# Shifted values copied as 112 rows and the rest, and the first batch's norm and turn by halves

## The chip, the cores and the metric

The kernel runs on one core of a Trainium2 chip. The time is the device time of one execution in microseconds (us); lower is better. In the core, TensorE (PE, with its weight load PEld), VectorE (DVE), ScalarE (ACT) and GpSimd (POOL) each run their own queue of instructions in order. SyncE (SP) issues all the DMAs here. The queues wait for each other through semaphores, which the kernel writes by hand.

## The reference

x is 4 batches of 1024 tokens of 128 channels, in float32. Cut to what matters here:

```python
h  = layernorm(x)
a  = h + ripple(h, Wqkv, Wo, conv_w)        # attention
x  = x + layernorm(a)
x  = x + layernorm(ffn(layernorm(x)))       # 8 experts, top 2, and a shared one

# ripple, per head of 16 channels (8 heads):
q, k, v = split(h @ Wqkv)
offsets = [0, 1, 2, 4, 8, 16, 32, 64, 128, 256, 512]    # earlier tokens that exist
w    = softmax over the offsets of q[s] . k[s - off] / 4
tele = sum over the offsets of w[off] * v[s - off]
conv = causal depthwise convolution of v, 7 taps
low  = elu features: fq @ (fk^T v) / (fq . sum fk)
out  = (tele + conv + low) @ Wo
```

The term `tele` needs, for each token s, the values of the tokens s - 1, s - 2, up to s - 64. The change touches how these shifted values are fetched, and how the first `layernorm(x)` of batch 0 is computed.

## The kernel before, in words

Tokens lie in 8 tiles of 128: tile j has its 128 tokens on the 128 partitions, so `x_in`, `xn`, `v_tok` are [128, 8, 128] (partition, tile, channel), 4 KB in each partition. Channel-major copies ([128 channels, 1024 tokens]) have names that end in T: `xnT`, `kT`, `qT`, `vT`.

**Batch by batch.** Each engine runs a loop over b = 0 to 4. In turn b the attention of batch b is computed, and beside it the feed-forward part of batch b-1 by units u of 512 tokens, and the normalising, turning and projecting of batch b+1. Batch 0 has no feed-forward beside it, so its stretch (about 19 to 87 us of the trace) is the attention of batch 0 and the preparation of batch 1.

**The start.** SP issues `x_in` first. DVE's `stats(0)` (L739, L743) takes mean and variance of the 8 tiles, POOL's `ln1(0)` turns them into `rstd1` by a power (L420) and into `nmr1` (L429), ACT's `normalise1(0)` (L502) writes `xn` in 8 instructions. PE's `turn_x` (L1081) transposes 4 tiles into each half of the PSUM tile `psA`; ACT's `evacuate_x` (L490) copies each half to `xnT`; PE projects k, q and v (L1089), each in two halves through the same `psA`, and ACT evacuates each. Before `turn_x(0)` PE runs 28 transposes that keep it busy (L1275). DVE's next work after `stats(0)` is `products(0, 0)` (L260), which waits for `qT`.

**The shifted values.** A token's value 1 to 64 tokens earlier lies on another partition, which the engines can't reach in an elementwise operation. So, once `v_tok` of a batch is evacuated, SP copies it by DMA from SBUF to SBUF into `v_shift` [128, 7, 8, 128], one slot for each offset in `SHIFTS` = 1, 2, 4, 8, 16, 32, 64 (`shift_v`, L333 to L337). For an offset `off` one DMA moves 128 - off partitions down by `off` (L336), 4 KB for each partition, and a second one takes the last `off` partitions of each tile to the first `off` partitions of the next tile (L337):

```python
sp.dma_start(v_shift[off:P, n], v_tok[0:P - off]).then_inc(v_shifted, 16)
sp.dma_start(v_shift[0:off, n, 1:NT], v_tok[P - off:P, 0:NT - 1]).then_inc(v_shifted, 16)
```

That is 14 DMAs and 3.60 MB in a batch. All of them count on one semaphore, and DVE waits for the full count once in each batch, ahead of the first tile of `weigh` (j = 0, L840). `weigh` multiplies the values by the softmax weights, tile by tile, into a ring of 4 buffers (`terms`); PE's `sum_terms` (L1166, L1169) sums them in `psH`, `add_conv` (L871, DVE) adds the convolution after tiles 4 and 7, PE applies `Wo` (L1180). DVE reaches `weigh` after products, features, convolution (`convolve`, L862, L864) and softmax of the batch.

**SP's queue.** Its order is fixed: in turn b the load of `x_in` for b+1, the 14 shift copies of b, a store, the reload of `x_res`, a store. Nothing that comes later is issued while an earlier issue stalls.

Of the kernel before, what the change touches and what calls it, by code (L numbers as in the profile page):

```python
# [16 lines left out]
ALU = mybir.AluOpType  # L17
# [3 lines left out]
P = 128  # L21
# [23 lines left out]
SHIFTS = TERMS[M_SHIFT:M_LOW]  # L45
# [7 lines left out]


N_DMA = 16
N_SHIFT_DMA = 16 * 2 * len(SHIFTS)
N_PSA_FULL, N_PSA_FREE = 16, 14

PSA_V_TOK, PSA_FK_TOK, PSA_SCORES, PSA_SCORES_T, PSA_X, PSA_K, PSA_Q, PSA_V = range(8)
PSA_AHEAD = 2 * 4  # L60
N_PRODUCTS = (4, 8, 11)
N_SOFTMAX_STEPS = 5
N_CONV_STEPS = TAPS

N_FRONT = 3
# [47 lines left out]
def block_kernel(nc, x, Wqkv, Wo, conv_w, gate_W, W1, b1, W2, b2, Ws1, bs1, Ws2, bs2, route_scale, out):  # L113
# [4 lines left out]
    with ExitStack() as ctx:  # L118
# [6 lines left out]
        def sem(name):  # L125
            return ctx.enter_context(nc.semaphore(name))
# [14 lines left out]
        neg_half = sb("neg_half", [P, NT])  # L141
# [11 lines left out]
        x_in = sb("x_in", [P, NT, P])  # L153
# [149 lines left out]
        def _(sp):  # L303
# [28 lines left out]
            def shift_v(b):  # L332

                sp.wait_ge(psA_free, freed(b, PSA_V_TOK, 1))
                for n, off in enumerate(SHIFTS):
                    sp.dma_start(v_shift[off:P, n], v_tok[0:P - off]).then_inc(v_shifted, 16)  # L336
                    sp.dma_start(v_shift[0:off, n, 1:NT], v_tok[P - off:P, 0:NT - 1]).then_inc(v_shifted, 16)  # L337

            def store(u):
# [24 lines left out]
        def _(pool):  # L364
# [51 lines left out]
            def rstd_of(var, src, scale, rstd, step, value, cols):  # L416

                nc.gpsimd.tensor_scalar(var[:, cols], src, scale, EPS, ALU.mult, ALU.add).then_inc(step, 1)  # L418
                pool.wait_ge(step, value)
                return nc.gpsimd.tensor_tensor(rstd[:, cols], var[:, cols], neg_half[:, cols], ALU.pow)  # L420

            def ln1(b):
                pool.wait_ge(stats1, upto(b, 1, 1))
                if b >= 3:
                    pool.wait_ge(ln3_ready, 2 * (b - 2))
                nc.gpsimd.tensor_scalar(neg_mean[:, b % 3, :], mv[:, :, 0], -1.0, 0.0, ALU.mult, ALU.add)
                rstd_of(var1, mv[:, :, 1], 1.0, rstd1, ln1_step, upto(b, 2, 1), slice(0, NT)).then_inc(ln1_step, 1)
                pool.wait_ge(ln1_step, upto(b, 2, 2))
                nc.gpsimd.tensor_tensor(nmr1[:], neg_mean[:, b % 3, :], rstd1[:], ALU.mult).then_inc(ln1_ready, 1)  # L429

            def ln2(u):
# [24 lines left out]
                nc.gpsimd.tensor_tensor(y_out[:, tiles, :], y_out[:, tiles, :], x2[:, tiles, :],  # L456
                                        ALU.add).then_inc(out_ready[0], TPH)

            ln1(0)
            constants()  # L460
            more_constants()
            for b in range(B + 1):
# [25 lines left out]
        def _(act):  # L488
# [6 lines left out]
                copy(dst, psA[:, half, :]).then_inc(psA_free, 1)  # L495

            def normalise1(b, tiles=range(NT)):
                act.wait_ge(ln1_ready, upto(b, 1, 1))
                if b:
                    act.wait_ge(xn_kept, upto(b - 1, 1, 1))  # L500
                for j in tiles:
                    nc.scalar.activation(xn[:, j, :], x_in[:, j, :], ACT.Identity, bias=nmr1[:, j:j + 1],  # L502
                                         scale=rstd1[:, j:j + 1]).then_inc(xn_ready, 1)

# [6 lines left out]
            def evacuate_x(b):  # L511
                for half in range(2):
                    evacuate(b - 1, PSA_X, half, xnT[:, bass.ts(half, HALF)])
# [214 lines left out]
        def _(dve):  # L728
# [4 lines left out]
            nc.vector.memset(hid[32:HID, 4, :], 0.0)  # L733
            nc.vector.memset(ksum_sel[:], 0.0).then_inc(zeros_set, 1)

            def stats(b):
                dve.wait_ge(x_in_ld, upto(b, N_DMA, 16))
                for j in range(NT):
                    last = nc.vector.bn_stats(bn[:, j, :], x_in[:, j, :])  # L739
                last.then_inc(bn_done, 1)  # L740
                dve.wait_ge(bn_done, upto(b, 1, 1))
                for j in range(NT):
                    last = nc.vector.bn_aggr(mv[:, j, :], bn[:, j, :])  # L743
                last.then_inc(stats1, 1)
# [661 lines left out]
```

## Time and profile before

| | |
|---|---|
| median of 3 runs | 334.6 us (333.72 to 335.88) |
| profiled execution | 334.57 us, its span 332.9 us |
| DVE busy | 269.8 us, 81% of the span |
| PE, PE load | 253.2 us, 172.3 us |
| ACT, POOL | 176.6 us, 72.1 us |
| mean granted clock of TensorE | 0.892 of full speed |
| data moved by DMA | 21.88 MB, mean 66 GB/s |

All the views show one profiled execution; 1.7 us of its time lie outside the span. The page's fourth part follows the chain of work that ended last back from the last instruction, and gives its share by line. A timeline gives each group of instructions with start, length and the idle time of its engine before it, with what ended that (`<-`). "SPq" is SP's queue: its rows are the issues of DMAs, not the transfers. In the view by stretches, PEclk is the granted clock of TensorE (1.00 is 2.4 GHz, 0.50 is 1.2 GHz), and the DMA share is the mean busy share of the core's 16 DMA engines: one engine of sixteen busy all the time is 0.06.

### The profile page before, as it was taken

How to read it: one execution, taken by the hardware profiler on the slowest of the kernel's cores; microseconds unless marked ns; L12 is line 12 of the kernel's file. 1: busy time of each engine (PE TensorE's matmuls, PEld its weight loads, DVE VectorE, ACT ScalarE, POOL GpSimd, SP SyncE). 2: the span in 40 equal slices, each digit the busy share in tenths (PEclk: the TensorE clock that was granted, in tenths of full speed). 3: DMA queues.
4: the chain of work that ended last, by engine and by line, in shares of the span. 5: the costliest groups of instructions: out<-in, count | busy, mean ns of one | idle time of the engine just before them, and what ended most of it. 6: DMA issues, size and time to landing. Idle time of an engine off the chain costs nothing.

```text
span 332.9 us, 4518 instructions
## 1 busy us (share of the span) xinstructions
PE 253.2 (76%) x1527; PEld 172.3 (52%) x1527; DVE 269.8 (81%) x595; ACT 176.6 (53%) x443; POOL 72.1 (22%) x129
## 2 busy tenths in 40 slices
PE   6668772088589939997898469997797588878894
PEld 6324340087436615776655228767444266675374
DVE  5079996088997999979989999889989989855752
ACT  1683256002536945584769625785478306176851
POOL 4903000001091000302492000221910003131013
PEclk9787979559959987999999959999999569999999
DMA  8200368000024720030038510100248301000003
GB/s 225 70 0 17 99 170 184 26 3 3 4 67 125 213 77 16 0 95 3 19 111 201 156 44 2 32 2 6 78 123 207 103 17 32 0 2 1 1 2 95
DMA packets 20037, 21.88 MB, mean 66 GB/s; under 512 B 3289, under 2 KB 16434, under 8 KB 20014
## 3 DMA queue, kind: packets, MB, share of 16 engines
q1 hardware_dynamic: 20014, 21.59, 23.5%
q8 instruction: 12, 0.20, 0.2%
q14 instruction: 11, 0.09, 0.1%
HBM read 5.07 MB, written 2.10 MB: 22 GB/s over the span
## 4 chain that ended last, share of the span: by engine, by line
PE 32%; DVE 22%; SPq 14%; ACT 12%; DMA 10%; POOL 4%; issue 3%; POOLq 0%; DVEq 0%; ACTq 0%
DMA v_shift<-v_tok 9%; SPq L337 9%; PE psH L1169 7%; PE psA L1089 6%; SPq L336 6%; DVE convT L864 5%; DVE prods L840 3%; PE psY L1266 3%; PE psF L1230 3%; PE psY L1180 2%; POOL rstd L420 2%; ACT xn L576 2%; DVE hid L968 2%; POOL var L418 2%; PE psA L1081 2%
## 5 line engine op out<-in xcount | busy, mean ns | idle before, releaser
L418 POOL TENSOR_SCALAR var<-ss 128x4 f32<-128x4 f32 (+1 forms) x25 | 13.2, 527 | 233.9 <-ACT squares L621 113.6
L260 DVE TENSOR_TENSOR prods<-qT,kT 128x1024 f32<-128x1024 f32 (+1 forms) x44 | 48.8, 1165 | 12.5 <-ACT qT L490 12.5
L1169 PE MATMUL psH<-ident,prods 128*128 128x128 f32 x324 | 42.8, 284 | 0.0
L1169 PEld LDWEIGHTS psH<-ident,prods 128*128 128x128 f32 x324 | 39.0, 148 | 2.3 <-issue 2.3
L420 POOL TENSOR_TENSOR rstd<-var,neg_half 128x4 f32<-128x4 f32 (+2 forms) x29 | 37.8, 1302 | 2.4
L840 DVE TENSOR_TENSOR prods<-v_shift,wgt 128x896 f32<-128x896 f32 x32 | 34.6, 1083 | 0.0
L864 DVE SCALAR_TENSOR_TENSOR convT<-vT,cw,convT 128x1024 f32<-128x1024 f32 x24 | 30.8, 1284 | 0.7
L1137 PE MATMUL psA<-prods,slot_sel 128*32 128x512 f32 x168 | 25.9, 671 | 7.3 <-DVE prods L260 5.3
L840 DVE TENSOR_TENSOR prods<-v_tok,wgt 128x128 f32<-128x128 f32 (+2 forms) x60 | 21.9, 391 | 11.6 <-DMA v_shift<-v_tok 11.6
L1089 PE MATMUL psA<-xnT,wqkv 128*128 128x512 f32 x48 | 28.8, 742 | 3.3 <-ACT xnT L490 3.3
L1230 PE MATMUL psF<-x3T,w 128*128 128x512 f32 x58 | 31.0, 647 | 0.1
L968 DVE TENSOR_TENSOR hid<-hid,psG 128x512 f32<-128x512 f32 x32 | 20.8, 683 | 8.3 <-PE psG L1252 7.3
L1166 PE MATMUL psH<-ident,prods 128*128 128x128 f32 x32 | 9.7, 304 | 20.8 <-DVE prods L840 17.2
L1252 PE MATMUL psG<-gT,gate_sel 24*128 24x512 bf16 x32 | 11.7, 421 | 17.2 <-DVE hid L968 15.7
L563 ACT ACTIVATE squares<-yc 128x128 f32<-128x128 f32 x32 | 9.4, 296 | 27.8 <-DVE yc L877 27.8
L598 ACT ACTIVATE hid<-psF,b1c 128x512 f32<-128x512 f32 x29 | 18.8, 685 | 2.8 <-PE psF L1230 2.7
L1266 PEld LDWEIGHTS psY<-w,hid 128*128 128x128 f32 x140 | 17.5, 205 | 4.2 <-DVE prods L824 3.6
L1266 PE MATMUL psY<-w,hid 128*128 128x128 f32 x140 | 17.7, 289 | 1.7 <-DVE prods L824 1.7
L1166 PEld LDWEIGHTS psH<-ident,prods 128*128 128x128 f32 x32 | 4.7, 147 | 26.5 <-DVE prods L840 21.6
L1089 PEld LDWEIGHTS psA<-xnT,wqkv 128*128 128x128 f32 x48 | 10.2, 237 | 15.2 <-ACT xnT L490 5.8
L1230 PEld LDWEIGHTS psF<-x3T,w 128*128 128x128 f32 x58 | 10.6, 205 | 13.5 <-issue 12.7
L502 ACT ACTIVATE xn<-x_in,nmr,rstd 128x128 f32<-128x128 f32 x32 | 12.9, 484 | 7.1 <-POOL nmr L429 7.1
(192 smaller groups left out, 520.3 us busy)
## 6 DMA issues: line engine op xcount, KB each, us to landing
x_in<-L_attn_x SPq DMA_DIRECT2D x4, 512.0 KB, 3.8
x_res<-L_attn_x SPq DMA_DIRECT2D x4, 512.0 KB, 15.6
v_shift<-v_tok SPq DMA_DIRECT2D x4, 508.0 KB
v_shift<-v_tok SPq DMA_DIRECT2D x4, 504.0 KB
v_shift<-v_tok SPq DMA_DIRECT2D x4, 496.0 KB
v_shift<-v_tok SPq DMA_DIRECT2D x4, 480.0 KB
v_shift<-v_tok SPq DMA_DIRECT2D x4, 448.0 KB
out<-y_out SPq DMA_DIRECT2D x7, 256.0 KB, 2.3
```

The lines of the kernel that those rows point to most:

```text
L260: return eng.tensor_tensor(prods[:, QUADS * (s % 2) + q, t0:T], qT[:, t0:T], kT[:, PRE - off + t0:PRE - off + T], ALU.mult)
L336: sp.dma_start(v_shift[off:P, n], v_tok[0:P - off]).then_inc(v_shifted, 16)
L337: sp.dma_start(v_shift[0:off, n, 1:NT], v_tok[P - off:P, 0:NT - 1]).then_inc(v_shifted, 16)
L420: return nc.gpsimd.tensor_tensor(rstd[:, cols], var[:, cols], neg_half[:, cols], ALU.pow)
L840: return nc.vector.tensor_tensor(dst, src.rearrange("p m (h d) -> p m h d", d=HD), w, ALU.mult)
L864: conv_chain(nc.vector.scalar_tensor_tensor(out=convT[:], in0=v, scalar=w, in1=convT[:], op0=ALU.mult, op1=ALU.add))
L968: nc.vector.tensor_tensor(hid[:, c, cols], hid[:, c, cols], psG[:, c % 2, :], ALU.mult).then_inc(gated, 1)
L1089: pe.matmul(psA[:, half, :], wqkv[:, bass.ts(part, P)], xnT[:, bass.ts(half, HALF)], start=True, stop=True).then_inc(psA_full, 1)
L1137: ins = pe.matmul(psA[32 * q:32 * q + 32, half, :], ksum_sel[:] if low else slot_sel[:, s, :], fqT[:, cols] if low else prods[:, QUADS * ( ...
L1169: ins = pe.matmul(dst, terms[:, j % TERM_BUFS, m, :], ident[:], is_transpose=True, start=False, stop=(m == live[-1]))
L1230: pe.matmul(hidden_bank(u, c), w1[:, bass.ts(c, P)], x3T[:, half_cols(u)], start=True, stop=True).then_inc(hidden_full, 1)
L1266: ins = pe.matmul(output_tile(u, n), hid[:, c, bass.ts(j, P)], w2[:, c, :], start=(c == CH - 1), stop=(c == CH - 2))
```

## The change

Two parts.

**The shift copies.** Where an offset leaves more than 112 partitions to move (offsets 1, 2, 4 and 8), the first of its DMAs is cut into one of 112 partitions and one of the rest (15, 14, 12 or 8). Offset 16 has 112, and 32 and 64 have fewer, so they stay. A batch has 18 copies in place of 14, of the same bytes; the count that DVE waits for is raised with them.

**The first batch's norm.** DVE's `first_norm` replaces `stats(0)`: by halves of 4 tiles it takes the statistics and adds epsilon (`var1`), POOL takes only the power of each half (`first_rstds`), DVE computes `nmr1` of each half and later `neg_mean`, and ACT normalises each half when its `nmr1` is there. DVE, not ACT, copies the two halves of the turned x from PSUM to `xnT`. Batches 1 to 3 are normalised as before, with the counts on their semaphores moved down by one.

```diff
-N_SHIFT_DMA = 16 * 2 * len(SHIFTS)
+SHIFT_ROWS = 112
+N_SHIFT_DMA = 16 * sum(3 if P - off > SHIFT_ROWS else 2 for off in SHIFTS)
@@ SP, shift_v
                 for n, off in enumerate(SHIFTS):
-                    sp.dma_start(v_shift[off:P, n], v_tok[0:P - off]).then_inc(v_shifted, 16)
+                    rows = min(SHIFT_ROWS, P - off)
+                    sp.dma_start(v_shift[off:off + rows, n], v_tok[0:rows]).then_inc(v_shifted, 16)
+                    if off + rows < P:
+                        sp.dma_start(v_shift[off + rows:P, n], v_tok[rows:P - off]).then_inc(v_shifted, 16)
                     sp.dma_start(v_shift[0:off, n, 1:NT], v_tok[P - off:P, 0:NT - 1]).then_inc(v_shifted, 16)
@@ POOL
+            def first_rstds():
+                for half in range(2):
+                    cols = slice(half * TPH, (half + 1) * TPH)
+                    pool.wait_ge(first_var, half + 1)
+                    nc.gpsimd.tensor_tensor(rstd1[:, cols], var1[:, cols], neg_half[:, cols],
+                                            ALU.pow).then_inc(first_rstd, 1)
...
-            ln1(0)
+            first_rstds()
             constants()
@@ ACT
             def normalise1(b, tiles=range(NT)):
-                act.wait_ge(ln1_ready, upto(b, 1, 1))
                 if b:
+                    act.wait_ge(ln1_ready, upto(b - 1, 1, 1))
                     act.wait_ge(xn_kept, upto(b - 1, 1, 1))
                 for j in tiles:
+                    if b == 0 and j % TPH == 0:
+                        act.wait_ge(first_normed, j // TPH + 1)
...
             normalise1(0)
-            evacuate_x(0)
+            act.wait_ge(psA_free, freed(-1, PSA_X, 1))
             evacuate_k(0)
@@ DVE
+            def first_norm():
+
+                dve.wait_ge(x_in_ld, N_DMA)
+                first_chain.start(dve, 0)
+                for half in range(2):
+                    tiles = range(half * TPH, (half + 1) * TPH)
+                    cols = slice(half * TPH, (half + 1) * TPH)
+                    for j in tiles:
+                        last = nc.vector.bn_stats(bn[:, j, :], x_in[:, j, :])
+                    first_chain(last)
+                    for j in tiles:
+                        last = nc.vector.bn_aggr(mv[:, j, :], bn[:, j, :])
+                    first_chain(last)
+                    nc.vector.tensor_scalar(var1[:, cols], mv[:, cols, 1], EPS, None, ALU.add).then_inc(first_var, 1)
+                for half in range(2):
+                    cols = slice(half * TPH, (half + 1) * TPH)
+                    dve.wait_ge(first_rstd, half + 1)
+                    nc.vector.scalar_tensor_tensor(out=nmr1[:, cols], in0=mv[:, cols, 0], scalar=-1.0,
+                                                   in1=rstd1[:, cols], op0=ALU.mult,
+                                                   op1=ALU.mult).then_inc(first_normed, 1)
+                nc.vector.tensor_scalar(neg_mean[:, 0, :], mv[:, :, 0], -1.0, None, ALU.mult)
+                for half in range(2):
+                    dve.wait_ge(psA_full, filled(-1, PSA_X, half))
+                    nc.vector.tensor_copy(xnT[:, bass.ts(half, HALF)], psA[:, half, :]).then_inc(psA_free, 1)
...
-            stats(0)
+            first_norm()
             dve.wait_ge(consts_ready, 1)
```

SP's queue from the load of batch 1's `x_in` on, before (127x1024 is 127 partitions of 1024 float32):

```order
L326 DMA x_in<-L_attn_x 128x8x128
L336 DMA v_shift<-v_tok 127x1024
L337 DMA v_shift<-v_tok 1x16x56
L336 DMA v_shift<-v_tok 126x1024
L337 DMA v_shift<-v_tok 2x896
```

and with the change:

```order
L331 DMA x_in<-L_attn_x 128x8x128
L342 DMA v_shift<-v_tok 112x1024
L344 DMA v_shift<-v_tok 15x1024
L345 DMA v_shift<-v_tok 1x16x56
L342 DMA v_shift<-v_tok 112x1024
L344 DMA v_shift<-v_tok 14x1024
L345 DMA v_shift<-v_tok 2x896
L342 DMA v_shift<-v_tok 112x1024
```

The copy of 127 partitions is now one of 112 and one of 15, that of 126 one of 112 and one of 14; the small copies behind them are as they were.

DVE's queue from its last memset to the features of batch 0, before:

```order
L734 MEMSET ksum_sel 128x32
L739 BN_STATS bn<-x_in 128x6 x8
L743 BN_AGGR mv<-bn 128x2 x8
L260 TENSOR_TENSOR prods<-qT,kT 128x1024 x4
L765 SCALAR_TENSOR_TENSOR fkT,ksum<-kexp,fkT 128x1024
```

and with the change (`nmr` is `nmr1`, `var` is `var1`):

```order
L751 MEMSET ksum_sel 128x32
L761 BN_STATS bn<-x_in 128x6 x4
L764 BN_AGGR mv<-bn 128x2 x4
L766 TENSOR_SCALAR var<-mv 128x4
L761 BN_STATS bn<-x_in 128x6 x4
L764 BN_AGGR mv<-bn 128x2 x4
L766 TENSOR_SCALAR var<-mv 128x4
L770 SCALAR_TENSOR_TENSOR nmr<-mv,rstd 128x4 x2
L773 TENSOR_SCALAR neg_mean<-mv 128x8
L776 COPY xnT<-psA 128x512 x2
L265 TENSOR_TENSOR prods<-qT,kT 128x1024 x4
L807 SCALAR_TENSOR_TENSOR fkT,ksum<-kexp,fkT 128x1024
```

DVE has seven instructions more ahead of the products: two `var`, two `nmr`, one `neg_mean` and two copies to `xnT`. The statistics come in groups of four tiles.

## Rows read from the trace of the kernel before

**Rows 1.** The page: busy time of each engine, and the chain by line.
```profile
PE 253.2 (76%) x1527; PEld 172.3 (52%) x1527; DVE 269.8 (81%) x595; ACT 176.6 (53%) x443; POOL 72.1 (22%) x129
...
DMA v_shift<-v_tok 9%; SPq L337 9%; PE psH L1169 7%; PE psA L1089 6%; SPq L336 6%; DVE convT L864 5%; DVE prods L840 3%; PE psY L1266 3%; PE psF L1230 3%; PE psY L1180 2%; POOL rstd L420 2%; ACT xn L576 2%; DVE hid L968 2%; POOL var L418 2%; PE psA L1081 2%
```

**Rows 2.** Timeline of DVE (start us, us, engine, line, tiles, idle before).
```profile
55.01 0.68 DVE L824 TENSOR_TENSOR prods<-psY,wgt 128x512 f32<-128x512 f32 x1
66.59 0.29 DVE L840 TENSOR_TENSOR prods<-v_tok,wgt 128x128 f32<-128x128 f32 x1 [10.90 <-DMA v_shift<-v_tok]
...
75.52 0.69 DVE L871 TENSOR_TENSOR prods<-psH,convT 128x512 f32<-128x512 f32 x1 [1.48 <-PE psH L1169]
...
269.56 0.29 DVE L840 TENSOR_TENSOR prods<-v_tok,wgt 128x128 f32<-128x128 f32 x1 [0.71 <-DMA v_shift<-v_tok]
```

**Rows 3.** Timeline of SP's queue, batch 0: the shift copies' issues.
```profile
25.97 0.73 SPq L336 DMA_DIRECT2D v_shift<-v_tok  x1
26.74 8.11 SPq L337 DMA_DIRECT2D v_shift<-v_tok  x1
...
50.44 1.05 SPq L337 DMA_DIRECT2D v_shift<-v_tok  x1
```

**Rows 4.** Stretches: length, busy us of each engine, PEclk, DMA share, GB/s.
```profile
core 0: us, PE busy (x) PEld busy (x) DVE busy (x) ACT busy (x) POOL busy (x), PEclk, DMA share, GB/s
13.30:16.50 3.20, 3.20 (x7) 1.37 (x6) 0.00 (x0) 1.23 (x3) 3.06 (x21) 0.61 0.56 164
28.00:34.80 6.80, 4.45 (x36) 2.42 (x32) 6.73 (x14) 0.81 (x1) 2.64 (x4) 0.89 0.07 26
50.40:55.70 5.30, 1.77 (x4) 0.30 (x2) 5.12 (x7) 4.65 (x6) 0.00 (x0) 1.00 1.06 230
57.70:66.50 8.80, 0.00 (x0) 0.00 (x0) 0.00 (x0) 0.00 (x0) 0.00 (x0) 0.50 0.06 26
66.70:74.50 7.80, 6.56 (x34) 6.56 (x35) 7.34 (x14) 0.00 (x0) 0.00 (x0) 0.54 0.01 3
89.50:97.50 8.00, 4.82 (x21) 1.38 (x21) 7.96 (x22) 4.81 (x21) 6.04 (x8) 0.59 0.07 22
```

**Rows 5.** DVE's convolution, 36 to 44 us and 48 to 57 us (busy, mean ns).
```profile
L864 DVE SCALAR_TENSOR_TENSOR convT<-vT,cw,convT 128x1024 f32<-128x1024 f32 x2 | 2.6, 1284 | 0.1
...
L864 DVE SCALAR_TENSOR_TENSOR convT<-vT,cw,convT 128x1024 f32<-128x1024 f32 x2 | 2.6, 1285 | 0.1
```

**Rows 6.** Timeline of the start, all engines.
```profile
3.06 6.13 PE L1275 MATMUL psG<-ident 128*128 128x128 f32 x28 [3.06 <-POOL ident L374]
...
4.24 1.64 DVE L739 BATCH_NORM_STATS2 bn<-x_in 128x6 f32<-128x128 f32 x8 [0.69 <-DMA x_in<-L_attn_x]
...
5.92 0.64 DVE L743 BATCH_NORM_AGGREGATE mv<-bn 128x2 f32<-128x6 f32 x8
...
7.20 1.66 POOL L420 TENSOR_TENSOR rstd<-var,neg_half 128x8 f32<-128x8 f32 x1
...
9.18 3.19 ACT L502 ACTIVATE xn<-x_in,nmr,rstd 128x128 f32<-128x128 f32 x8 [7.11 <-POOL nmr L429]
...
10.97 0.64 PE L1081 MATMUL psA<-ident,xn 128*128 128x128 f32 x4 [1.78 <-ACT xn L502]
...
12.42 1.11 PE L1081 MATMUL psA<-ident,xn 128*128 128x128 f32 x4 [0.81 <-ACT xn L502]
...
18.28 0.60 ACT L490 ACTIVATE qT<-psA 128x512 f32<-128x512 f32 x1 [0.36 <-PE psA L1089]
...
19.02 4.63 DVE L260 TENSOR_TENSOR prods<-qT,kT 128x1024 f32<-128x1024 f32 x4 [12.46 <-ACT qT L490]
```

**Rows 7.** Timeline of POOL: two powers of four columns.
```profile
81.29 1.19 POOL L420 TENSOR_TENSOR rstd<-var,neg_half 128x4 f32<-128x4 f32 x1
...
91.76 1.86 POOL L420 TENSOR_TENSOR rstd<-var,neg_half 128x4 f32<-128x4 f32 x1
```

**Rows 8.** Waits of the whole span: us in total, times, longest.
```profile
DVE prods L840 <- DMA v_shift<-v_tok: 11.6, 2, 10.9
```

More of the change, by code:

```diff
@@ L62 @@
 N_SOFTMAX_STEPS = 5
+N_FIRST_STEPS = 4
 N_CONV_STEPS = TAPS
@@ L228, in block_kernel @@
         bn_done = sem("bn_done")
+        first_step, first_var = sem("first_step"), sem("first_var")
+        first_rstd, first_normed = sem("first_rstd"), sem("first_normed")
         ln1_ready, ln2_ready, ln3_ready, ln4_ready = sem("ln1_ready"), sem("ln2_ready"), sem("ln3_ready"), sem("ln4_ready")
@@ L250, in block_kernel @@
         softmax_chain = Chain(softmax_step, N_SOFTMAX_STEPS)
+        first_chain = Chain(first_step, N_FIRST_STEPS)
         conv_chain = Chain(conv_step, N_CONV_STEPS)
@@ L420, in rstd_of @@
                 return nc.gpsimd.tensor_tensor(rstd[:, cols], var[:, cols], neg_half[:, cols], ALU.pow)
+            def first_rstds():
[4 more added lines that the diff above has]
+                                            ALU.pow).then_inc(first_rstd, 1)
             def ln1(b):
-                pool.wait_ge(stats1, upto(b, 1, 1))
+                pool.wait_ge(stats1, upto(b - 1, 1, 1))
                 if b >= 3:
@@ L426, in ln1 @@
                 nc.gpsimd.tensor_scalar(neg_mean[:, b % 3, :], mv[:, :, 0], -1.0, 0.0, ALU.mult, ALU.add)
-                rstd_of(var1, mv[:, :, 1], 1.0, rstd1, ln1_step, upto(b, 2, 1), slice(0, NT)).then_inc(ln1_step, 1)
-                pool.wait_ge(ln1_step, upto(b, 2, 2))
+                rstd_of(var1, mv[:, :, 1], 1.0, rstd1, ln1_step, upto(b - 1, 2, 1), slice(0, NT)).then_inc(ln1_step, 1)
+                pool.wait_ge(ln1_step, upto(b - 1, 2, 2))
                 nc.gpsimd.tensor_tensor(nmr1[:], neg_mean[:, b % 3, :], rstd1[:], ALU.mult).then_inc(ln1_ready, 1)
@@ L734, in _ @@
             nc.vector.memset(ksum_sel[:], 0.0).then_inc(zeros_set, 1)
+            def first_norm():
[21 more added lines that the diff above has]
+                    nc.vector.tensor_copy(xnT[:, bass.ts(half, HALF)], psA[:, half, :]).then_inc(psA_free, 1)
             def stats(b):
-                dve.wait_ge(x_in_ld, upto(b, N_DMA, 16))
+                dve.wait_ge(x_in_ld, upto(b, N_DMA, N_DMA))
                 for j in range(NT):
@@ L740, in stats @@
                 last.then_inc(bn_done, 1)
-                dve.wait_ge(bn_done, upto(b, 1, 1))
+                dve.wait_ge(bn_done, upto(b - 1, 1, 1))
                 for j in range(NT):
```

## The prediction

> **What bounds the kernel now.** I read the page first. DVE is the busiest engine, 81% of the span, and on the chain that ended last the transfers to `v_shift` have 9% and their issues on SP (L336, L337) another 15% [rows 1]. So the next question is where DVE waits for them. The view of waits gives two such waits and 11.6 us for the whole program [rows 8]; the timeline of DVE places them. In batch 0 DVE is through with its last work ahead of `weigh` at 55.69 (55.01 + 0.68) and starts the first tile at 66.59, after 10.90 us of idling. In batch 3 it idles 0.71 us at the same place, in batches 1 and 2 not at all [rows 2].
>
> Then the transfers themselves. SP issues the first copy of batch 0 at 25.97 and the last at 50.44, and one issue alone takes 8.11 us [rows 3]: the queue stalls. The view by stretches tells why. From 28.0 to 34.8 and again from 57.7 to 66.5 the DMA share is 0.07 and 0.06, one engine of sixteen, and 26 GB/s move. In between, from 50.4 to 55.7, all engines are busy and 230 GB/s move. Batch 1 shows the same thin stretch at 89.5 to 97.5 [rows 4]. A copy of 127 partitions is 127 x 4 KB = 0.52 MB; at 26 GB/s it takes 20 us. That fits one engine carrying all of the copy for offset 1, first alone with the queue blocked behind it, and at the end alone again.
>
> **The change, part by part.**
>
> *The copies.* The bytes stay at 3.60 MB in a batch, the DMAs go from 14 to 18. If the 112-partition piece runs on all sixteen engines (7 partitions each), and the rest of 15, 14, 12 or 8 on that many, no engine has much more than its sixteenth, and 3.60 MB at 230 GB/s [rows 4] take 15.7 us. Each new issue costs SP 0.7 us [rows 3], four in a batch, on a queue that has nothing late behind it; I take nothing for it, since it lies inside the 15.7 us. With the start 2 us earlier (below) the first issue comes at 24.0; allowing 5 us for starting and landing, all is there by 45. DVE arrives at 55.7 - 2.0 = 53.7. The cover is 9 us, and the transfers could run as slowly as 3.60 MB in 29.7 us, 121 GB/s, before DVE waited again. So the wait of batch 0 goes whole: **10.9 us**. That of batch 3 too: **0.7 us**. Batches 1 and 2 give nothing. Next in line behind the copies at that place is DVE's own work, which is busy without a gap up to there, so nothing else is late.
>
> Here a rule speaks against the change. The thin stretches show one engine at work on one copy and sixteen on many [rows 4]. The Trainium skill (DMA: Bandwidth & Descriptors, Rules for kernel authors) says not to bother with two transfers to disjoint halves of the partitions, since both run over the same sixteen engines and serialise. By that rule the split would give nothing; it is a rival below. The same page, in Why a DMA increments its semaphore by 16 and not by 1, has a rule that says the opposite for these sizes: the number of engines is the largest up to 16 that divides the partition count, which is 1 for 127, 14 for 126, 4 for 124 and 16 for 112. By that rule (the trace agrees: a share of 0.06 while the first copy runs) rival A falls.
>
> *The PE behind it.* After its 15.8 us of idling PE summed the first tiles at a granted clock of 0.54 (66.7 to 74.5) and DVE's `add_conv` waited 1.48 us for it [rows 2, 4]. Now PE has work again some 5 us after its last projection in place of 16. The clock may not fall, or come back earlier. Between 0 and 1.5 us; I take **1.0**, as the idling is a third of what it was.
>
> *The start.* Before, x lands, DVE takes the statistics from 4.24 (1.64 us) and aggregates from 5.92 (0.64), POOL does two small steps up to 7.20, a power of 8 columns (1.66) and one more step, and ACT begins at 9.18 and ends at 12.37 [rows 6]. The two small steps from 6.56 to 7.20 cost 0.3 us each; I take that for each `var1` and `nmr1`. By halves: statistics 0.82, aggregation 0.32, `var1` 0.3, 0.1 between them: the first half's `var1` is there at 5.8, the second's at 7.3. POOL's power of 4 columns costs 1.19 us, or 1.86 where DVE was busy beside it [rows 7]: 7.0 to 7.65. With `nmr1` ACT starts at 7.6 to 7.95, and its four tiles take 1.6 us. The second power ends at 8.55 to 9.5 and its `nmr1` at 8.85 to 9.8, so ACT ends at 10.8 to 11.4, in place of 12.37. PE's warm-up ends at 9.19, and the first turn (0.64 us) follows as soon as its tiles are there [rows 6]; DVE's copy of that half (0.68 us, as its other operation of 512 columns from PSUM [rows 2]) is done before the second turn is. The projection of k, which started at 13.53 behind the second turn (12.42 + 1.11), starts at 11.5 if that turn takes 0.64 us, and at 12.5 if ACT is late and it takes 1.11. That is 1.0 to 2.0 us. From 13.3 to 16.5 PE projected at a clock of 0.61 [rows 4]; at full clock 39% of these 3.2 us, 1.2 us, would go too. DVE starts its products when `qT` is there (it had idled 12.46 us) [rows 6], so all of it is on the path. Between 1.0 and 3.2; I take the middle of the two sizes and half of the clock's, **2.0**.
>
> What the start adds to DVE (two `var1`, two `nmr1`, `neg_mean`, two copies: at most 2.9 us) lies in those 12.46 idle us. The cover stays as long as the copies are not late: if DVE were held up there, `xnT` would be later by the same time. ACT loses two copies of 0.6 us; the projection no longer waits for it. POOL's constants start about 1 us earlier. The load of x of batch 1 goes out 2 us earlier and still long before its statistics.
>
> *Sum.* 10.9 + 0.7 + 1.0 + 2.0 = 14.6 us. From this execution's 334.57 us (span 332.9) that is 320.0 us; the median of the runs is 334.6, so it stands for both. What is behind batch 0 moves as one block: the waits there are between engines that all come earlier, none is for a fixed time.
>
> **The rivals.**
>
> *A. The pieces serialise, and the landing stays where it is.* Then only the start's 2.0 us are won, as `v_tok` and all behind it come earlier: 332.6 us. For it speaks the rule named above. Against it, 230 GB/s in the stretch where many copies run together [rows 4], which a single engine's 26 GB/s can't give. 4%.
>
> *B. The transfers spread, but at half the rate* (many pieces of 4 KB and under, more issues). At 100 GB/s they take 36 us and with 2 us for starting and landing are there at 62; DVE waits 8.3 us in place of 10.9, and none in batch 3, as the copies took 40.6 us before (25.97 to 66.57 in batch 0): 334.6 - 2.6 - 0.7 - 2.0 = 329.3 us. For it: nothing but the rise from 14 to 18. Against it, the same 230 GB/s were reached by the copies of 112 and fewer partitions, which don't change. 3%.
>
> *C. The start gives nothing,* since POOL and DVE slow each other in their small steps (the power at 1.86 [rows 7] in both halves, the turn at half clock): 322.0 us. 8%; it lies in the range.
>
> *D. Slower: the transfers now run at full rate beside DVE and slow it.* Before, a good part of each batch's transfer time had one engine at work; now 16 us in each batch run at 230 GB/s, under DVE's products. This is the one mechanism that could turn the sign: 4 x 16 = 64 us of DVE work would have to stretch by (14.6 + 3.3) / 64, 28%, to give 338 us. Against it, the convolution took 1284 ns each at 36 to 44 us and 1285 at 48 to 57, where 230 GB/s moved [rows 4, 5]. 2%.
>
> **How the numbers follow.** The forecast has 83%, A 4%, B 3%, C 8%, D 2%. The range: all terms at their best, 10.9 + 0.7 + 1.5 + 3.2 = 16.3, give 318.3, and some 1.8 us below that for a clock that falls into other stretches of the batches (0.59 at 89.5 to 97.5 [rows 4]); at their worst, 11.6 + 0 + 1.0 = 12.6, they give 322.0, with 2 us above it for the same: 316.5 to 324. What a measurement here can tell from no change is about 1%, 3.3 us. Forecast, B and C are faster by more: 94%. A is within it: 4%. D is slower: 2%.
>
> **What would show it.** In the changed kernel's trace DVE should start `weigh` of batch 0 near 54 us without a wait for `v_shift`; the first copies of a batch should show a DMA share near 1 instead of 0.06, no issue on SP should take 8 us, and the last packet should land some 20 us after the first issue. ACT's first `xn` should start near 7.8, k's projection near 11.5, DVE's products near 17. PEclk in the first tiles of `sum_terms` should be above 0.54. A landing after 54 us, or a thin stretch of one engine, would prove the first term wrong; a first product after 18 us the last one.

## The result, and the profile after

Median 322.57 us (322.11 to 324.78, 4 runs) against 334.21 us (333.72 to 335.88, 4 runs) of the kernel before: ratio 0.9656, 95% interval 0.9600 to 0.9713. Forecast was 320.0 us, range 316.5 to 324. The profiled execution of the changed kernel took 322.11 us, its span is 320.4 us. Here and below ratios leave out a run that is over 1.5% above the fastest of its kernel and in that counts as slow; there is one, in experiment 1.

The page of the changed kernel, its first part and the chain by line:

```profile
PE 253.8 (79%) x1527; PEld 171.8 (54%) x1527; DVE 269.2 (84%) x602; ACT 175.7 (55%) x441; POOL 73.3 (23%) x127
...
PE psH L1211 9%; DVE convT L906 9%; PE psA L1131 6%; PE psY L1308 5%; DVE prods L265 5%; PE psF L1272 4%; PE psY L1222 3%; ACT xn L593 3%; POOL rstd L428 2%; DVE hid L1010 2%; PE psG L1294 2%; DVE top L847 2%; ACT squares L586 2%; POOL var L426 2%; DVE prods L913 2%
```

`v_shift` and its issues, 24% of the chain before [rows 1], are no longer among its lines. DVE has 84% of the span, PE is on the chain with its `sum_terms` (L1211).

The timeline of DVE, the places of [rows 2] and the start of the products [rows 6], then `add_conv` (L913) in batches 1 and 2:

```profile
15.53 5.09 DVE L265 TENSOR_TENSOR prods<-qT,kT 128x1024 f32<-128x1024 f32 x4 [3.76 <-ACT qT L505]
...
52.58 0.28 DVE L882 TENSOR_TENSOR prods<-v_tok,wgt 128x128 f32<-128x128 f32 x1
...
60.77 0.69 DVE L913 TENSOR_TENSOR prods<-psH,convT 128x512 f32<-128x512 f32 x1 [0.74 <-PE psH L1211]
...
129.47 0.69 DVE L913 TENSOR_TENSOR prods<-psH,convT 128x512 f32<-128x512 f32 x1 [2.97 <-PE psH L1211]
...
201.35 0.69 DVE L913 TENSOR_TENSOR prods<-psH,convT 128x512 f32<-128x512 f32 x1 [2.79 <-PE psH L1211]
```

The products start at 15.53 in place of 19.02. `weigh` of batch 0 starts at 52.58 with no idling in front of it, where it started at 66.59 after 10.90 us of it. But `add_conv` of batches 1 and 2 now waits 2.97 and 2.79 us for PE. The same two of the kernel before:

```profile
143.08 0.69 DVE L871 TENSOR_TENSOR prods<-psH,convT 128x512 f32<-128x512 f32 x1 [0.45 <-PE psH L1169]
...
214.23 0.69 DVE L871 TENSOR_TENSOR prods<-psH,convT 128x512 f32<-128x512 f32 x1 [0.92 <-PE psH L1169]
```

The timeline of SP's queue in batch 0, first two issues and the last, against [rows 3]:

```profile
21.78 0.58 SPq L342 DMA_DIRECT2D v_shift<-v_tok  x1
22.40 0.92 SPq L344 DMA_DIRECT2D v_shift<-v_tok  x1
...
34.44 0.60 SPq L345 DMA_DIRECT2D v_shift<-v_tok  x1
```

No issue stalls; the last one is at 34.44, 12.7 us after the first. It was 24.5 us. By stretches, against [rows 4]:

```profile
core 0: us, PE busy (x) PEld busy (x) DVE busy (x) ACT busy (x) POOL busy (x), PEclk, DMA share, GB/s
24.00:35.00 11.00, 8.84 (x58) 4.07 (x50) 10.90 (x26) 1.37 (x2) 2.64 (x4) 0.84 0.82 248
51.50:58.30 6.80, 4.38 (x21) 4.38 (x22) 6.80 (x14) 1.06 (x1) 0.00 (x0) 0.50 0.00 0
...
106.00:116.30 10.30, 7.38 (x13) 3.27 (x14) 9.89 (x18) 3.77 (x7) 0.00 (x0) 0.50 0.01 2
116.40:121.30 4.90, 4.90 (x42) 4.60 (x41) 4.69 (x19) 1.16 (x2) 0.00 (x0) 1.00 0.00 0
```

From 24 to 35 the share is 0.82 and 248 GB/s move, where it was 0.07 and 26 GB/s. The lower three rows are for PE's clock; experiments 6 and 7 show that it is the reason for the waits at `add_conv`. In batch 1 it stood at 0.50 from 106.0 to 116.3, 10.3 us. The same low stretch of the kernel before is 6.6 us long:

```profile
core 0: us, PE busy (x) PEld busy (x) DVE busy (x) ACT busy (x) POOL busy (x), PEclk, DMA share, GB/s
...
121.70:128.30 6.60, 4.27 (x10) 1.93 (x11) 6.36 (x9) 1.77 (x4) 0.00 (x0) 0.50 0.06 26
```

The start, all engines, against [rows 6, 7]:

```profile
5.75 1.02 POOL L434 TENSOR_TENSOR rstd<-var,neg_half 128x4 f32<-128x4 f32 x1 [2.75 <-DVE var L766]
...
7.15 3.19 ACT L519 ACTIVATE xn<-x_in,nmr,rstd 128x128 f32<-128x128 f32 x8 [5.08 <-DVE nmr L770]
...
10.38 0.66 PE L1123 MATMUL psA<-ident,xn 128*128 128x128 f32 x4 [0.82 <-ACT xn L519]
...
14.80 0.60 ACT L505 ACTIVATE qT<-psA 128x512 f32<-128x512 f32 x1 [0.36 <-PE psA L1131]
```

Along the program the two profiles stand so (start in us, before and after): products of batch 0 19.02 and 15.53, 3.5 won; DVE free for `weigh` 55.69 and 52.58, 3.1; `weigh` starts 66.59 and 52.58, 14.0; `add_conv` of batch 0 75.52 and 60.77, 14.75; `add_conv` of batch 1 143.08 and 129.47, 13.6; of batch 2 214.23 and 201.35, 12.9; the whole execution 12.5. So the gain was there by 76 us, 0.15 us more than the whole forecast; 2.3 us of it were given back in batches 1 to 3, and so were the 0.7 us of batch 3's wait for `v_shift`, which went too: 3.0 us in all.

### The profile page after: what moved, and what is told of

Read it like the earlier page. It is cut to its first block, busy times and chain, and to the rows that moved or that the text cites. A ratio compares the mean times of both kernels' runs of the same rounds, so it can differ in the third digit from the quotient of the medians.

```text
span 320.4 us, 4538 instructions
## 1 busy us (share of the span) xinstructions
PE 253.8 (79%) x1527; PEld 171.8 (54%) x1527; DVE 269.2 (84%) x602; ACT 175.7 (55%) x441; POOL 73.3 (23%) x127
## 4 chain that ended last, share of the span: by engine, by line
PE 41%; DVE 36%; ACT 13%; POOL 5%; issue 3%; DMA 1%; POOLq 0%; DVEq 0%; ACTq 0%
PE psH L1211 9%; DVE convT L906 9%; PE psA L1131 6%; PE psY L1308 5%; DVE prods L265 5%; PE psF L1272 4%; PE psY L1222 3%; ACT xn L593 3%; POOL rstd L428 2%; DVE hid L1010 2%; PE psG L1294 2%; DVE top L847 2%; ACT squares L586 2%; POOL var L426 2%; DVE prods L913 2%
## 5 line engine op out<-in xcount | busy, mean ns | idle before, releaser
L426 POOL TENSOR_SCALAR var<-ss 128x4 f32<-128x4 f32 (+1 forms) x25 | 11.9, 475 | 223.2 <-ACT squares L638 114.9
L1211 PE MATMUL psH<-ident,prods 128*128 128x128 f32 x324 | 43.7, 287 | 0.0
L1211 PEld LDWEIGHTS psH<-ident,prods 128*128 128x128 f32 x324 | 39.8, 150 | 2.3 <-issue 2.3
L428 POOL TENSOR_TENSOR rstd<-var,neg_half 128x4 f32<-128x4 f32 (+2 forms) x28 | 36.3, 1298 | 2.3
L1272 PE MATMUL psF<-x3T,w 128*128 128x512 f32 x58 | 32.9, 683 | 0.1
L1131 PE MATMUL psA<-xnT,wqkv 128*128 128x512 f32 x48 | 26.7, 692 | 3.3 <-ACT xnT L505 3.3
L882 DVE TENSOR_TENSOR prods<-v_tok,wgt 128x128 f32<-128x128 f32 (+2 forms) x60 | 20.8, 373 | 0.0
L1272 PEld LDWEIGHTS psF<-x3T,w 128*128 128x128 f32 x58 | 11.4, 218 | 14.9 <-issue 14.0
L1208 PE MATMUL psH<-ident,prods 128*128 128x128 f32 x32 | 9.8, 306 | 10.2 <-DVE prods L882 7.7
L1131 PEld LDWEIGHTS psA<-xnT,wqkv 128*128 128x128 f32 x48 | 8.9, 212 | 13.8 <-ACT xnT L505 5.0
L519 ACT ACTIVATE xn<-x_in,nmr,rstd 128x128 f32<-128x128 f32 x32 | 12.9, 484 | 5.1 <-DVE nmr L770 5.1
L1294 PEld LDWEIGHTS psG<-gT,gate_sel 24*128 24x128 bf16 x32 | 2.2, 93 | 23.4 <-DVE hid L1010 20.0
```

The source lines that it names most:

```text
L882: return nc.vector.tensor_tensor(dst, src.rearrange("p m (h d) -> p m h d", d=HD), w, ALU.mult)
L1131: pe.matmul(psA[:, half, :], wqkv[:, bass.ts(part, P)], xnT[:, bass.ts(half, HALF)], start=True, stop=True).then_inc(psA_full, 1)
L1211: ins = pe.matmul(dst, terms[:, j % TERM_BUFS, m, :], ident[:], is_transpose=True, start=False, stop=(m == live[-1]))
L1272: pe.matmul(hidden_bank(u, c), w1[:, bass.ts(c, P)], x3T[:, half_cols(u)], start=True, stop=True).then_inc(hidden_full, 1)
L1294: pe.matmul(psG[:, c % 2, :], gate_sel[:, c, :], gT[:, u % 2, :], start=True, stop=True).then_inc(gate_spread, 1)
```

## The experiments

Ratios are to the kernel before in the same session on the same chip, with 95% intervals.

**1. The copies alone.** Kernel before, with this of the change:

```diff
-                    sp.dma_start(v_shift[off:P, n], v_tok[0:P - off]).then_inc(v_shifted, 16)
+                    rows = min(SHIFT_ROWS, P - off)
+                    sp.dma_start(v_shift[off:off + rows, n], v_tok[0:rows]).then_inc(v_shifted, 16)
+                    if off + rows < P:
+                        sp.dma_start(v_shift[off + rows:P, n], v_tok[rows:P - off]).then_inc(v_shifted, 16)
```

> The kernel before with the 112-row copies alone; the start is the old one. Theory (one engine carried the copy of 127 partitions): DVE's waits for v_shift of 10.9 and 0.7 us go, 11.6 us, plus up to 1 us at the first add_conv, minus some 2.5 us that PE's clock may cost in batches 1 and 2: ratio 0.966 to 0.975, 322 to 326 us. Rival A (pieces serialise): the wait stays at 10 us or more, ratio 0.99 to 1.00.

Measured: 327.19 us (323.74 to 328.67, 4 runs), ratio 0.9697 (0.9608 to 0.9785). The ratio is of three of the runs, whose median is 325.83 us; ratio and this median are as expected, the median of all four is 1 us above the range. Rival A falls: DVE has no wait for `v_shift` any more. It waited 1.02, 3.06, 2.82 and 1.14 us at the first `add_conv` of batches 0 to 3, and 2.44 us for the scores of batch 0, all for PE. The long waits of batches 1 to 3 stand here with the old start, and experiment 2 has at most 1.22 us there with the new one: the giving back comes with the copies, not with the new start.

**2. The start alone.** The changed kernel with the old copies:

```diff
-N_SHIFT_DMA = 16 * sum(3 if P - off > SHIFT_ROWS else 2 for off in SHIFTS)
+N_SHIFT_DMA = 16 * 2 * len(SHIFTS)
-                    sp.dma_start(v_shift[off:off + rows, n], v_tok[0:rows]).then_inc(v_shifted, 16)
-                    if off + rows < P:
-                        sp.dma_start(v_shift[off + rows:P, n], v_tok[rows:P - off]).then_inc(v_shifted, 16)
+                    sp.dma_start(v_shift[off:P, n], v_tok[0:P - off]).then_inc(v_shifted, 16)
```

> The changed kernel with the shift copies put back to 127, 126, 124 and 120 partitions; only the start is new. Theory: DVE's products start at 15.5 us in place of 19.0, and all behind them, the copies too, so the kernel wins 3 to 3.5 us, ratio 0.990; DVE still waits some 10.9 us at weigh of batch 0. Rival: the start's gain is lost before weigh or in the clock, ratio 0.995 to 1.00.

Measured: 331.98 us (330.49 to 333.96, 10 runs), ratio 0.9900 (0.9869 to 0.9932), as expected. DVE's `weigh` of batch 0 in its timeline:

```profile
62.62 0.29 DVE L878 TENSOR_TENSOR prods<-v_tok,wgt 128x128 f32<-128x128 f32 x1 [8.62 <-DMA v_shift<-v_tok]
```

The copies land at 62.6 in place of 66.6, 4.0 us earlier: the start is passed on whole. The wait is 8.62 and not 10.9 us, since in this execution DVE itself came later to `weigh`, by 1.36 us of waiting for PE at the scores; as long as a transfer ends the wait, that costs nothing. By the ratios the two parts alone win 10.2 us (7.2 to 13.2) and 3.4 us (2.3 to 4.4), 13.5 together; the whole won 11.6 and, in experiment 7, 10.9. Within the first interval that is the same; more can't be said of whether the parts add up.

**3. Cuts at 113 partitions.** Is it the number of pieces, or the number of engines for each?

```diff
-SHIFT_ROWS = 112
+SHIFT_ROWS = 113
```

> The changed kernel with cuts at 113 partitions in place of 112: offsets 1, 2, 4 and 8 become 113 and 14, 13, 11, 7. As many copies, nearly the same sizes. Theory (the engine count is a divisor of the partition count; 113 has none, so each of four copies runs on one engine): 4 x 113 x 4 KB at 26 GB/s is 71 us on one engine in each batch, DVE waits 45 to 55 us in every batch, the kernel takes over 450 us, DMA share near 0.06 for most of it. Rival (what helps is the number of pieces, or that none is over 120 partitions): as the change, 320 to 326 us.

Measured (one run): 484.28 us. The view of waits, the timeline of SP's queue and a stretch of batch 0:

```profile
DVE prods L882 <- DMA v_shift<-v_tok: 168.0, 4, 49.7
```

```profile
29.64 0.66 SPq L342 DMA_DIRECT2D v_shift<-v_tok  x1
30.34 16.08 SPq L344 DMA_DIRECT2D v_shift<-v_tok  x1
```

```profile
95.00:105.00 10.00, 1.05 (x5) 1.06 (x6) 2.40 (x5) 0.00 (x0) 0.00 (x0) 0.50 0.06 22
```

Four waits, one in each batch, 42 us on average and 49.7 the longest (45 to 55 had been expected), issues that stall 16 us, one engine's share of 0.06 and 22 GB/s. As many copies as the change has, each large one smaller than the whole ones before, and 162 us slower. The partition count of the piece decides; that it is a piece gives nothing. Here a rule of the Trainium skill (DMA: Bandwidth & Descriptors, Why a DMA increments its semaphore by 16 and not by 1) can be named: a DMA runs on the largest number of engines up to 16 that divides the partition count. By it 112 partitions have 16 engines and 113 have 1, and the runs agree: a share of 0.82 and 248 GB/s in batch 0 of the change, 0.06 and 22 GB/s here.

**4. Only the copy of 127 partitions cut.** The changed kernel with

```diff
-N_SHIFT_DMA = 16 * sum(3 if P - off > SHIFT_ROWS else 2 for off in SHIFTS)
+N_SHIFT_DMA = 16 * (2 * len(SHIFTS) + 1)
-                    rows = min(SHIFT_ROWS, P - off)
+                    rows = SHIFT_ROWS if off == 1 else P - off
```

> The changed kernel with only the copy of 127 partitions cut (112 and 15); 126, 124 and 120 stay whole. Theory (the engine count is the largest divisor up to 16: 14, 4 and 15 for these): the busiest engine has about 83 pieces of 4 KB in a batch, 13 us at 26 GB/s, so the copies are there by 45 us, DVE doesn't wait, and the time is that of the change within 1 us. Rival (all four cuts are needed): DVE waits for v_shift by several us in batch 0.

Measured: 324.10 us (323.58 to 324.93), ratio 0.9681 (0.9635 to 0.9727), beside 324.32 us of the change in the same session. Same within the noise, no wait for `v_shift`. By stretches (columns as above):

```profile
22.00:37.00 15.00, 11.12 (x63) 6.23 (x64) 14.86 (x34) 2.35 (x4) 2.65 (x4) 0.73 0.59 161
37.00:41.00 4.00, 3.87 (x32) 2.03 (x31) 1.48 (x3) 2.03 (x5) 0.00 (x0) 0.97 0.89 252
```

The copies are slower at first, a share of 0.59 where the change has 0.82, and last until about 42 us, under the cover that ends at 53. Three of the four cuts buy nothing here. The one cut is worth some 7 us: ratio 0.9681 with it, 0.9900 without any (experiment 2).

**5. The copies to `xnT` back on ACT.** The changed kernel with `evacuate_x(0)` on ACT in place of DVE's two copies:

```diff
-            act.wait_ge(psA_free, freed(-1, PSA_X, 1))
+            evacuate_x(0)
@@ DVE, first_norm
-                for half in range(2):
-                    dve.wait_ge(psA_full, filled(-1, PSA_X, half))
-                    nc.vector.tensor_copy(xnT[:, bass.ts(half, HALF)], psA[:, half, :]).then_inc(psA_free, 1)
```

> The changed kernel with ACT, not DVE, copying the turned x to xnT in batch 0. Theory (the halves' norm gives the start's gain, the engine of the copies gives nothing much): ACT is free of xn at 10.4 us, its first copy ends at 11.0 and the second at 11.7, k's first matmul starts at most 0.2 us later, DVE's products start within 0.3 us of 15.5. Rival (the copies on DVE are needed): the products start 0.8 us later or more.

Measured (one run): 324.37 us. The timeline of its ACT and DVE:

```profile
10.49 0.57 ACT L505 ACTIVATE xnT<-psA 128x512 f32<-128x512 f32 x1
11.33 0.60 ACT L505 ACTIVATE xnT<-psA 128x512 f32<-128x512 f32 x1 [0.27 <-PE psA L1120]
...
15.69 5.12 DVE L265 TENSOR_TENSOR prods<-qT,kT 128x1024 f32<-128x1024 f32 x4 [7.01 <-ACT qT L505]
```

and DVE of the change in the same session:

```profile
15.82 5.09 DVE L265 TENSOR_TENSOR prods<-qT,kT 128x1024 f32<-128x1024 f32 x4 [3.77 <-ACT qT L505]
```

No loss, as far as one run and one profile tell. ACT is through with the first copy at 11.06, before the second turn ends at 11.30. The start's gain comes from the halves, not from the engine of the copies.

**6. PE kept busy.** The open question was the 2.3 us given back. In batches 1 to 3 PE idles some 5 us ahead of the projections, as it waits for DVE's gated hidden values; it then runs the projections, hidden layers and `experts_out` that stand in its queue ahead of `sum_terms`. In this kernel transposes of the identity, whose result nobody reads, fill that time:

```diff
+FILL_FIRST = 18
+FILL_GATES = 32
@@ PE
                         gate_logits(u1)
+                        keep_busy(FILL_GATES, psF[:, psF_bank(u1, LOGITS), :])
                         spread_gates(u0, range(2, 4))
...
                         project_q(b + 1)
+                        keep_busy(FILL_FIRST, psF[:, 0, :])
```

> The changed kernel with transposes of the identity into an unused bank in two places where PE idles: 18 after the last projection for batch 1 in turn 0, and 32 in each of turns 1 to 3 behind gate_logits(u1), where PE waits some 5 us for DVE's gated hidden values. Nothing else moves. Theory (the 2 to 3 us that are missing from the sum of the gains are lost since PE's granted clock is low when it comes back to work, so it reaches sum_terms late and DVE waits at add_conv, 2.97, 2.79 and 1.12 us in batches 1 to 3): those waits fall under 1 us, the clock is 1.00 there, and the kernel wins 3 to 6 us against the change: ratio to before 0.947 to 0.957, 316 to 320 us. Rival (the missing part has another cause, or the fills push PE's work later): waits as they were, ratio 0.965 or above.

Measured: 320.18 us (319.79 to 321.97), ratio 0.9569 (0.9511 to 0.9628), at the upper edge of what was expected. The wait at the first `add_conv` fell under 0.4 us in batches 1 and 3 and to 0.97 in batch 2. In batch 2 the fill was through 2.67 us before DVE was, and the clock fell still. The stretches of batch 1:

```profile
104.00:110.00 6.00, 4.50 (x36) 3.66 (x35) 5.86 (x7) 1.85 (x3) 0.00 (x0) 1.00 0.01 3
110.00:117.00 7.00, 6.23 (x21) 3.33 (x20) 6.76 (x14) 4.09 (x7) 0.00 (x0) 0.76 0.00 0
```

The clock is better (0.76 where the change had 0.55 from 110 to 117), but not full.

**7. Longer fills, and the change beside them.** The same with 46, (44, 54, 44), 20 more behind `linear_state` in batch 0, 6 behind `turn_logits(u1)` and 28 ahead of the last batch's `experts_out`:

```diff
+FILL_KEYS = 20
+FILL_FIRST = 46
+FILL_GATES = (0, 44, 54, 44)
+FILL_TURNED = 6
+FILL_LAST = 28
```

> As e3_fill, with the fills as long as PE's idle stretches there: 46 in place of 18 after the last projection in turn 0, 44, 54 and 44 in place of 32 in turns 1 to 3, and new ones of 20 in turn 0 behind linear_state, of 6 behind turn_logits(u1), and of 28 in turn 3 ahead of experts_out. Theory (a low clock after PE's idling costs DVE its waits): the clock is 1.00 through these stretches, DVE's waits at add_conv in batches 0 to 2 (0.42, under 0.4 and 0.97 us in e3_fill) and at the scores of batch 0 (1.37 us) shrink, and the kernel wins 1 to 4 us more: 316 to 319 us, ratio to before 0.945 to 0.955. Rival (the fills that are longer than the idling push PE): 320 us or more.

> The changed kernel once more, beside the others on one chip. Theory: ratio 0.962 to 0.970, and among its runs the slower ones have the lower mean clock. Against e5_fill_more it is 4 to 7 us slower.

Measured: 317.60 us (316.60 to 319.34), ratio 0.9492 (0.9448 to 0.9537), beside 324.32 us (321.08 to 325.32), ratio 0.9671 (0.9623 to 0.9719), of the change. PE, then the clock, then DVE's `add_conv` in batch 1:

```profile
100.82 4.97 PE L1322 MATMUL psF<-ident 128*128 128x128 f32 x44
```

```profile
104.00:110.00 6.00, 5.23 (x33) 3.55 (x32) 5.89 (x8) 1.72 (x4) 0.00 (x0) 1.00 0.00 0
110.00:117.00 7.00, 5.92 (x40) 4.50 (x39) 6.69 (x20) 3.20 (x5) 0.00 (x0) 1.00 0.01 2
```

```profile
125.76 0.69 DVE L918 TENSOR_TENSOR prods<-psH,convT 128x512 f32<-128x512 f32 x1 [0.21 <-PE psH L1216]
```

At full clock through the whole stretch, PE is in time and DVE waits 0.21 us in place of 3.06 in the change's own profile of that session; in batch 2 it waits 0.17 in place of 2.83. The change's runs bear the clock out, if not in every step: the run of 321.08 us had a mean clock of 0.904 and that of 322.89 had 0.906, those of 324.06 to 325.32 had 0.890.

Not all of the 6.7 us come from batches 1 to 3. The change's profile in this experiment has one more wait for PE, in batch 0, where the scores are ready late:

```profile
41.32 0.22 DVE L838 TENSOR_SCALAR zden<-psA 128x64 f32<-128x64 f32 x1 [2.54 <-PE psA L1123]
```

From 31.0 to 37.6 us its PEclk is 0.50. With the fills DVE waits 0.24 us there, and `add_conv` of batch 0 starts at 60.29 in place of 63.68: 3.4 us of the 8.4 between the two spans (315.2 and 323.6) are won by then. The profile of 322.11 us had no such low clock (1.00 from 28 to 51 us) and waited 0.24 us as well; the other profiles of the new copies without fills waited 2.1 to 2.5. So this wait comes and goes between executions of one kernel. It may be a part of why the change took 322.57 us in one session and 324.32 in another; only one run of each was traced.

**8. The same fills in the kernel before.** If the low clock is a cost that the change uncovered, the old kernel should gain little from them.

```diff
+FILL_GATES = (0, 44, 54, 44)
...
```

(the same edits, in the kernel before; its partner is the kernel of experiment 7 again)

> The kernel before, with the same fills as e5_fill_more. Theory (the change's terms add up, and what was missing from them is PE's low clock after idling, which costs the changed kernel some 5 us of DVE's waits and the one before under 2): the wait of 10.9 us for v_shift stays, the kernel wins only 1 to 2 us, 333 to 334.5 us, and the distance to the changed kernel with fills is 15 to 16.5 us, the whole sum of the terms, in place of the 11 to 12 without fills. Rival (the fills help any kernel alike): 5 to 7 us won, 329 us, distance 11 to 12 us.

> e5_fill_more once more, as the partner of e9_before_filled on one chip. Ratio to before 0.945 to 0.954, 316 to 319.5 us; DVE waits under 0.5 us at add_conv in batches 1 and 2.

Measured: 332.76 us (331.44 to 335.45, 12 runs), ratio 0.9942 (0.9911 to 0.9974), and 317.27 us (316.72 to 320.94), ratio 0.9498 (0.9450 to 0.9546), with waits of 0.23 and 0.18 us at `add_conv` of batches 1 and 2. So 2.1 us for the old kernel, a little more than expected, against 6.7 us for the changed one (experiment 7). Between the medians of the two filled kernels lie 15.5 us, by the ratios give or take 2; their two profiles are 17.5 us apart (spans of 332.5 and 315.0). The timeline of DVE in batch 0 of the old kernel with fills:

```profile
66.48 0.29 DVE L845 TENSOR_TENSOR prods<-v_tok,wgt 128x128 f32<-128x128 f32 x1 [10.85 <-DMA v_shift<-v_tok]
...
75.26 0.69 DVE L876 TENSOR_TENSOR prods<-psH,convT 128x512 f32<-128x512 f32 x1 [1.33 <-PE psH L1174]
```

The wait of 10.9 us stands there untouched.

## Why the prediction was right, and where a step failed

**The copies, 10.9 and 0.7 us: right.** Both waits are gone, and the reason was the one given: one engine carried the copy of 127 partitions. At 113 partitions (experiment 3), with four such copies, it came back about fourfold. The rate was 248 GB/s where 230 was taken, and the cover was even larger than thought: experiment 4 got along with one cut.

**PE behind it, 1.0 us: right in size for the forecast's profile** (1.48 to 0.74 us at `add_conv` of batch 0; the other profiles with the new copies and without fills have 0.85 to 1.06), but not by its mechanism. PE idled 6.26 us in place of 15.77, and the clock stood at 0.50 from 51.5 to 58.3 all the same. It took fills to end this wait.

**The start, 2.0 us: too small.** It was 3.5 us at the products and 3.1 at `weigh`. POOL's power of 4 columns took 1.02 us, not 1.19 to 1.86; `nmr1` and `var1` cost 0.15 to 0.17 and not 0.3, so that ACT began at 7.15 and not at 7.6 to 7.95; and PE's clock stood at 1.00 from 13 to 16 us, of which only half had been counted. 0.4 us were lost again behind it: the four products took 5.09 us in place of 4.63 [rows 6].

**"What is behind batch 0 moves as one block": this step failed.** The gain of 14.75 us at 76 us was 12.5 at the end. In batches 1 to 3 PE comes back from idling at a low clock, in the kernel before too; but there, in batch 1, the full clock came back 5.2 us after PE had work again (123.25 to 128.4), and in the changed kernel 8.2 us after (108.15 to 116.3), so the work in PE's queue ahead of `sum_terms` ends later and DVE waits. In batch 2 it came back 6.2 and 7.8 us after, in batch 3 9.8 and 10.2. There the low stretch is as long before as after (batch 2, before and after):

```profile
core 0: us, PE busy (x) PEld busy (x) DVE busy (x) ACT busy (x) POOL busy (x), PEclk, DMA share, GB/s
189.90:200.10 10.20, 5.44 (x11) 2.59 (x12) 9.86 (x13) 1.86 (x5) 0.00 (x0) 0.50 0.22 70
...
177.80:188.00 10.20, 6.99 (x13) 3.11 (x14) 9.82 (x16) 3.39 (x6) 0.00 (x0) 0.50 0.00 0
```

But PE has work again 4.0 us after it begins before (at 193.88) and 2.4 us after it begins with the change (at 180.23), so more of the work runs at half the clock.

In the kernels with fills that keep the clock up the sum comes out: 15.5 us between their medians, against 10.9 + 0.7 from the copies, 3.1 to 3.5 from the start and 0.7 from PE in batch 0, 15.4 to 15.8. Term by term it is less exact than that: the old kernel with fills had no wait for `v_shift` in batch 3 and 1.33 us at `add_conv` of batch 0, where the changed one had none, and the two profiles differ by 15.1 us there but by 16.7 in batch 1, behind a wait of 1.5 us for ACT's `gexp` that only the old kernel's profile has. The range had 1.8 to 2 us for a clock that falls elsewhere, as a margin; it was a term of its own. That the time still came out 2 to 3 us from the forecast is in part luck: the start's 1.1 to 1.5 us too little stood against the 3.0 us that were lost behind batch 0.

**Rival D, transfers that slow DVE: wrong by the direct comparison.** DVE's seven products beside the copies, before at a mean of 73 GB/s (share 0.22) and after at 254 (share 0.84):

```profile
30.37 7.50 DVE L260 TENSOR_TENSOR prods<-qT,kT 128x512 f32<-128x512 f32 x7
```

```profile
27.35 7.50 DVE L265 TENSOR_TENSOR prods<-qT,kT 128x512 f32<-128x512 f32 x7
```

7.50 us both times, and DVE's busy time as a whole is 269.2 us where it was 269.8. Rivals A and B fall with the share of 0.82, C with the 3.5 us.

**Where part of the waits was made good.** DVE waits 2.5, 1.9 and 1.1 us more than before at the first `add_conv` of batches 1 to 3, 5.5 us, but its busy time between these landmarks is 1.0 to 1.1 us less in each. In the kernel before POOL's addition to `y_out` runs beside DVE's work, and one DVE operation takes about 1 us longer there; in batch 1:

```profile
139.66 1.27 POOL L456 TENSOR_TENSOR y_out<-y_out,x 128x512 f32<-128x512 f32 x1 [1.32 <-ACT y_out L630]
139.76 1.20 DVE L959 CAST gparts<-gtmp 128x32 bf16<-128x32 f32 x1
```

In the changed kernel the addition starts 1.3 us after the cast, close to DVE's wait, which begins at 126.5; the cast takes 0.18 us, and it is POOL that takes longer:

```profile
124.65 0.18 DVE L1001 CAST gparts<-gtmp 128x32 bf16<-128x32 f32 x1
...
126.03 1.60 POOL L471 TENSOR_TENSOR y_out<-y_out,x 128x512 f32<-128x512 f32 x1 [1.96 <-ACT y_out L647]
```

Batches 2 and 3 show the same: before, two DVE products take 1.83 in place of 0.75 us (at 210.49) and the cast 1.27 (at 279.30); after, POOL's addition takes 1.79 and 2.18 us, and DVE's operations their usual time. With the longer fills, where DVE hardly waits, the cast takes 1.20 to 1.26 us again. So about 3 of the 5.5 us cost nothing: DVE had been held up there before, beside POOL, and was then held up by PE instead. What is left, 1.5, 0.7 and 0.1 us, is about half of how much later the clock came back in each batch (3.0, 1.6 and 0.4 us), which is what work at half the clock would lose; that is an estimate from these rows.

**What stays open.** Why the clock's return comes later against PE's work in the changed kernel. All five profiles of kernels with the new copies and without fills show the waits of about 3.0, 2.8 and 1.1 us in batches 1 to 3, and both profiles with the old copies and without fills 0.45 to 1.2 in batches 1 and 2. In those five DVE's wait at `add_conv` of batch 0 ends 2.2 to 2.5 us after the clock has come back, and `add_conv` of batch 1 follows 68.7 to 69.0 us later; so the next low stretch may fall in the same place each time. That is an argument; no run tried it.

## What to carry to other kernels

Count for each DMA how many engines its partition count gives it, before looking at its bytes: one copy of 127 partitions held back a batch's whole set, and one cut at 112 was worth some 7 us, while three further cuts were worth nothing, because they had cover already. Move a wait away, and ask what the next engine was doing during it: PE's idling in the other batches had been there all the time, and filling it was worth only 2.1 us until the other terms were gone; then transposes into a free bank were worth 6.7 us, and the two together are the fastest version here, 317.3 to 317.6 us. A gain found early in a program isn't a gain at its end: compare the same landmarks of both profiles batch by batch.

## What the runs showed of the hardware that was not expected

- One DMA engine moved 22 to 26 GB/s from SBUF to SBUF when it was alone (shares of 0.06 and 0.07); in stretches with most of the sixteen at work 230 to 254 moved, about 15 each.
- Behind a copy that runs on one engine SP's queue itself stalls: an issue that takes 0.6 to 0.9 us with the change took 8.1 us, and 16.1 to 16.8 at 113 partitions.
- The same kernel's runs spread along with TensorE's mean clock. Of eleven runs of the kernel before in one session, those with a mean granted clock of 0.897 took 333.1 to 334.4 us, those with 0.878 took 337.1 and 337.5. With the longer fills 0.984 gave 316.6 to 317.0, and 0.962 to 0.964 gave 318.2 to 319.3.
- POOL's `affine_select` of 24 x 512 and DVE's products took longer beside each other: three of them 3.11 us beside the products after the change, 2.27 alone before, and four products 5.09 in place of 4.63. All profiles with the new start have 5.08 to 5.12, all with the old one 4.63. With POOL's `y_out` addition only one of the two is longer: a small DVE cast (1.20 us in place of 0.18, the addition 1.27), or the addition (2.18 us, a DVE product beside it its usual 1.08).
